# A graph layer on one Trainium2 core: a home in SBUF for every gathered tile, and other unit sizes for its features

## The chip, the cores and the metric

The kernel runs on 1 core of one Trainium2 chip. The time is device microseconds of one execution of the whole program. The engines are called PE (TensorE), DVE (VectorE), ACT (ScalarE), POOL (GpSimd) and SP (SyncE, here only a queue of plain DMAs).

## The reference, cut to what matters

`x` has 100,000 nodes of 32 floats. There are 25,000 edges, sorted by their destination `dst`.

```python
h = relu(layernorm(x))                         # 100000 x 32
# node part: a product of every node's own features
out = x + concat(h[:, :8] @ Ws, einsum(h[:, 8:], Wv)) / sqrt(8)
# edge part
w = silu(silu(edge_attr_8 @ W1 + b1) @ W2 + b2) @ W3 + b3   # 25000 x 256
hs_e, hv_e = h[src]                            # gather of source rows
messages = tensor_product(hs_e, hv_e, edge_attr_4, w)       # 25000 x 32
out += segment_sum(messages, dst) / 4          # scatter with add
```

## The kernel before

It has two stages, and every engine runs its own program, tied to the others by semaphores.

**Node stage.** 50 chunks (48 of 128 partitions x 16 rows, two smaller ones). SP loads a chunk of `x` (`load_x`) and stores its result (`store`), PE, ACT and DVE work on it in `node_step(c, base, ...)`. `base` is the step; from step 8 on the steps are in a hardware loop of 8. In step `base`, DVE takes row sums of chunk `base + 2` if `base` is odd, and finishes chunk `base - 2` (`node_rstd`, `node_scale`, `node_add`). Ahead of step 8 DVE also scales the weights and makes a few constants.

**Gathers.** The edges are 196 tiles of 128. POOL fetches the source rows of one tile with one indirect DMA (`gather`, line 320): 128 rows of 128 bytes of `x` into `xg`. DVE and ACT turn gathered rows into features, unit by unit, in the steps `feat_sum` (writes `gsum`), `feat_centre` (writes `gc`), `feat_square`, `feat_var`, `feat_std`, `feat_rstd`, `feat_scale` (writes `h_all`). There are three buffers `xg`, and POOL waits for the `feat_centre` of the unit that used a buffer before it fills it again (`gc_done`). Units 0 to 11 have 10 tiles each, and a unit is summed in node step 4n + 4. Unit 12 has 17 tiles and is summed in the last steps of the node stage. The other units have 5 tiles (the last has 4), one for each pass of the edge stage. POOL gathers 147 tiles ahead of its first scatter, and 49 between the scatters.

**Edge stage.** 12 passes of 4 quads and one more quad: 49 quads (q = 0 to 48), each of 4 tiles. PE makes the weights `w` of a quad, DVE multiplies and sums (`products`, `sum_vectors`, `sum_scalars`, `outer_product`, `vectors`), PE adds up rows with one destination within a quad (`sum_batch`), ACT copies these sums out of PSUM (`copy_sums`, line 508) into one of `NS` = 4 buffers `sums`, DVE works out which rows are written and where (`index_rank` to `index_out`, line 1038 writes `idx_i`), and POOL adds them to `out` in DRAM with 4 indirect DMAs (`scatter`, line 351). A scatter's first DMA waits for `idx_done` of its quad and for the landing of three DMAs of the quad before; the second waits for the landing of the fourth, and a `nop` then signals `landed`. `copy_sums(q)` waits for `landed >= q - 2`, so the work on the quads can be some three quads ahead of POOL. Between the scatters of a pass POOL gathers 1, 1, 1 and 2 tiles. It starts to scatter only when all chunks are stored.

**SP's queue** is in order. At lines 274 and 275 it waits for `dst_pad`, which an `iota` on POOL gives (line 335, behind the 20th gather), and only then come the store of `spare0`, the first `store` and the load of chunk 8.

Of the kernel before, what the change touches and what calls it, by code (L numbers as in the profile page):

```python
# [19 lines left out]
def gnn_layer(nc, x, src, dst, edge_sh, edge_radial, W1, b1, W2, b2, W3, b3, Ws, Wv, out):  # L20
# [6 lines left out]
    P = 128  # L27
# [36 lines left out]
    GT, GM, GL = 10, 17, 5  # L64
    GF = EARLY * GT + GM
    assert GF + GL * (NU // 2 - 1) + BT == T + 1
    DR = D + 1
    BW = BT * P
    HL = (NU // 2 - 2) // 2
# [9 lines left out]
    with ctx:  # L79
# [43 lines left out]
        xg = [sb(f"xg{i}", [P, GM * D]) for i in range(3)]  # L123
        gsum = sb("gsum", [P, GM])
        gc = sb("gc", [P, GM * D])
        gsq = sb("gsq", [P, GM * D])
        gvar = sb("gvar", [P, GM])
        gstd = sb("gstd", [P, GM])
        grstd = sb("grstd", [P, GM])
        h_all = sb("h_all", [P, (T + 1) * D])  # L130
# [32 lines left out]
        def bank(b, n=1):  # L163
# [20 lines left out]
            sum_ready sums_done scattered scattered_last idxc_done carry_done erlast_loaded dve_zero b3_scaled""".split()  # L184
# [4 lines left out]
        gathered = [sem(f"gathered{i}") for i in range(3)]  # L189
# [10 lines left out]
        def unit_first(n):  # L200

            return GF + (n - EARLY - 1) * GL

        def unit_slot(odd):
            return 1 if odd else 2

        def unit_count(half, odd):

            return half * GL + (EARLY // 2 * GT + GL if odd else GL)
# [5 lines left out]
        def _(sp):  # L215
# [85 lines left out]
            def edge_pass(v):  # L301
# [5 lines left out]
            edge_pass(0)  # L307
            with sp.Fori(1, NU // 2 - 1) as v:
                edge_pass(v)
# [3 lines left out]
        def _(pool):  # L313
# [5 lines left out]
            def gather(t, i, slot):  # L319
                pool.indirect_dma_start(xg[slot][:, i * D:(i + 1) * D], None, x,  # L320
                                        bass.IndirectOffsetOnAxis(ap=src_all[:, t:t + 1], axis=0))\
                    .then_inc(gathered[slot], 16)

            pool.wait_ge(src_loaded, 16)
            for n in range(EARLY):
                if n >= 2:

                    pool.wait_ge(s["gc_done"], n - 1)
                for i in range(GT):
                    gather(n * GT + i, i, n % 2)  # L330
                if n == 1:
                    pool.iota(rank_w[:, :], pattern=[[1, 1]], base=(127 + 63) << 23, channel_multiplier=-(1 << 23))\
                        .then_inc(s["pool_const"], 1)
                    pool.iota(trash_i[:, :], pattern=[[P, BT]], base=N, channel_multiplier=1).then_inc(s["pool_const"], 1)
                    pool.iota(dst_i[:, T:T + 1], pattern=[[1, 1]], base=N + (BT - 1) * P, channel_multiplier=1)\
                        .then_inc(s["dst_pad"], 1)
# [29 lines left out]
            def edge_pass(v):  # L366

                n, slot = EARLY + 3 + v, unit_slot(v % 2)
                t0 = unit_first(n)
                tiles = max(0, min(GL, T + 1 - t0))  # L370
                if tiles > 0:
                    if t0 + tiles > T:
                        pool.wait_ge(srclast_loaded, 16)

                    pool.wait_ge(s["gc_done"], n - 1)
                for k in range(4):
                    for i in range(k * tiles // 4, (k + 1) * tiles // 4):
                        gather(t0 + i, i, slot)
                    scatter(4 * v + k, 4 * v + k)


# [3 lines left out]
            for v in range(NU // 2):  # L385
                edge_pass(v)
            scatter(NQ - 1, NQ - 1)
# [5 lines left out]
        def _(act):  # L393
# [71 lines left out]
            def node_step(c, base, i):  # L465
# [6 lines left out]
                if 4 <= base < FULL:  # L472
                    n = 2 * i + base % 8 // 4 - 1
                    if base % 4 == 1:
                        feat_square(n, GT)
                    if base % 4 == 3:
                        feat_std(n, GT)

                if base == FULL:
                    feat_square(EARLY - 1, GT)  # L480
                if base == FULL + 2:
                    feat_square(EARLY, GM)
                if base == FULL + 1:
                    feat_std(EARLY - 1, GT)
# [61 lines left out]
            feat_std(EARLY, GM)  # L546
# [9 lines left out]
            def edge_pass(v, first, last):  # L556
                n = EARLY + 1 + v
                for h in range(2):
# [8 lines left out]
                    if h == 0 and not first:  # L567
                        feat_std(n - 1, GL)
# [4 lines left out]
                    if h == 1:  # L573
                        feat_square(n, BT if last else GL)
# [606 lines left out]
```

## Time and profile before

| | |
|---|---|
| median of 3 runs | 660.89 us (660.28 to 661.85) |
| time of the profiled execution | 658.62 us |
| its span, first to last instruction | 656.7 us |
| mean granted TensorE clock in it | 0.809 |
| busy, share of the span | PE 80%, DVE 71%, ACT 59%, POOL 77% |
| gathers, scatter DMAs | 196, 196 |

The profile records one execution. The span is what the trace shows; 1.9 us of the execution's time lie outside it. A share of busy time is an average over two stages with different limits, and the chain of work that ended last tells which engine held up the end.

### The profile page before, as it was taken

Reading aid. Unit: us, or ns where it says so; the run is one execution under the profiler, and the core shown is the slowest. Engines: PE = TensorE matmul, PEld = TensorE weight load, DVE = VectorE, ACT = ScalarE, POOL = GpSimd, SP = SyncE. Lnnn points to the kernel's source line nnn. Section 1 sums busy time; section 2 is a strip of 40 time slices with the busy share of each in tenths; the row PEclk is TensorE's granted clock in tenths of the full one; section 3 lists DMA queues with packets and bytes.
Section 4 is the critical chain, followed back from the end, with each engine's and each line's share of the span. In section 5 each row is a group of like instructions: output and inputs, shape, how many; then the busy total and the mean of one; then the engine's idle time right before and its main releaser. Section 6 shows DMA issues by size and latency. Waiting matters only on the chain.

```text
span 656.7 us, 10632 instructions
## 1 busy us (share of the span) xinstructions
PE 523.2 (80%) x2843; PEld 397.3 (60%) x2867; DVE 465.9 (71%) x1137; ACT 388.4 (59%) x1107; POOL 505.1 (77%) x401
## 2 busy tenths in 40 slices
PE   6989999889239999888988888879898788887400
PEld 4878887778115766565666566656575556665400
DVE  5759986877238999987687677767688776786400
ACT  3435555554137898957586766667576866587300
POOL 5777777777770688888888888888888888888884
PEclk9859999899559989897768678887768778888555
DMA  4376675554110122222222222222222222222221
GB/s 120 97 234 197 197 207 175 162 170 138 46 31 4 10 13 12 12 12 11 12 11 12 9 12 11 12 12 11 12 11 11 11 10 9 10 10 11 8 9 6
DMA packets 54364, 33.95 MB, mean 52 GB/s; under 512 B 37942, under 2 KB 41928, under 8 KB 54344
## 3 DMA queue, kind: packets, MB, share of 16 engines
q0 software_dynamic: 34496, 6.45, 18.4%
q1 hardware_dynamic: 19784, 27.28, 12.4%
q8 instruction: 7, 0.11, 0.1%
q14 instruction: 13, 0.11, 0.1%
q10 hardware_dynamic: 64, 0.00, 0.0%
HBM read 17.60 MB, written 16.08 MB: 51 GB/s over the span
## 4 chain that ended last, share of the span: by engine, by line
POOL 36%; DMA 17%; issue 11%; DVE 4%; ACT 1%; PE 1%; POOLq 0%; DVEq 0%; ACTq 0%
POOL out_dram L351 35%; DMA out_dram<-sums,idx_i 17%; POOL xg L320 2%; DVE red L1059 1%; DVE prod L1050 1%; DVE prod L1046 1%; PE ps L683 0%; DVE msg L1066 0%; PE ps L669 0%; ACT dsq L520 0%; ACT eq L542 0%; DVE h_all L913 0%; ACT L434 0%; ACT L451 0%; DVE gc L897 0%
## 5 line engine op out<-in xcount | busy, mean ns | idle before, releaser
L351 POOL DMA_INDIRECT out_dram<-sums,idx_i x196 | 307.1, 1567 | 60.9 <-issue 52.0
L320 POOL DMA_INDIRECT xg<-in_x_dram,src_all x196 | 197.0, 1005 | 83.0 <-issue 56.0
L736 PE MATMUL ps<-msg,eq 128*128 128x32 f32 (+1 forms) x980 | 138.9, 304 | 3.8 <-ACT sums L508 2.6
L736 PEld LDWEIGHTS ps<-msg,eq 128*128 128x128 f32 x980 | 138.4, 227 | 4.0 <-issue 2.7
L683 PE MATMUL ps<-w3blk,x 128*128 128x512 f32 x196 | 125.6, 729 | 3.5 <-issue 2.8
L1059 DVE TENSOR_REDUCE red<-prod 128x128 f32<-128x1024 f32 x49 | 97.7, 1994 | 0.1
L520 ACT ACTIVATE dsq<-ps,dcol 128x512 f32<-128x512 f32 x196 | 87.1, 537 | 0.2 <-PE ps L695 0.2
L508 ACT ACTIVATE sums<-ps 128x132 f32<-128x132 f32 x49 | 13.7, 279 | 123.5 <-POOLq L361 99.9
L683 PEld LDWEIGHTS ps<-w3blk,x 128*128 128x128 f32 x196 | 46.0, 246 | 46.1 <-issue 41.5
L542 ACT ACTIVATE eq<-dsq,onecol 128x384 f32<-128x384 f32 x147 | 73.5, 520 | 0.0
L635 PEld LDWEIGHTS ps<-ones_g,sqT 128*128 128x128 f32 x392 | 53.7, 205 | 24.3 <-issue 17.1
L695 PEld LDWEIGHTS ps<-ident,dcol 128*128 128x128 f32 x196 | 23.8, 145 | 70.8 <-issue 59.0
L695 PE MATMUL ps<-ident,dcol 128*128 128x128 f32 x196 | 32.3, 290 | 42.1 <-ACT dsq L520 42.0
L1014 DVE SCALAR_TENSOR_TENSOR first<-sums,rank_max,dmt_all 128x4 f32<-128x4 f32 x49 | 10.7, 219 | 70.2 <-ACT sums L508 70.0
L639 PE MATMUL ps<-wself,rT 128*128 128x128 f32 x392 | 59.6, 298 | 0.0
L635 PE MATMUL ps<-ones_g,sqT 128*128 128x4 f32 x392 | 50.6, 252 | 9.9 <-ACT nstd L425 4.8
L417 ACT ACTIVATE sqT<-ps 128x512 f32<-128x512 f32 (+2 forms) x50 | 29.2, 584 | 42.4 <-PE ps L624 42.4
L1046 DVE TENSOR_TENSOR prod<-ps,coef 128x768 f32<-128x768 f32 x49 | 46.8, 954 | 10.2 <-PE ps L684 7.4
L1050 DVE TENSOR_TENSOR prod<-ps,coef 128x256 f32<-128x256 f32 x147 | 52.6, 413 | 0.0
L1066 DVE TENSOR_REDUCE msg<-prod 128x32 f32<-128x512 f32 x49 | 52.5, 1072 | 0.0
L639 PEld LDWEIGHTS ps<-wself,rT 128*128 128x128 f32 x392 | 50.9, 203 | 0.0
L669 PE MATMUL ps<-x,w2blk 128*128 128x512 f32 (+1 forms) x50 | 43.8, 973 | 3.3 <-ACT x L451 3.2
(102 smaller groups left out, 798.7 us busy)
## 6 DMA issues: line engine op xcount, KB each, us to landing
xin<-in_x_dram SPq DMA_DIRECT2D x48, 256.0 KB
out_dram<-oc SPq DMA_DIRECT2D x48, 256.0 KB, 2.1
xg<-in_x_dram,src_all POOLq DMA_INDIRECT x196, 2.4
out_dram<-sums,idx_i POOLq DMA_INDIRECT x196, 3.1
er<-in_edge_attr_dram SPq DMA_DIRECT2D x24, 32.0 KB
sh_all<-in_edge_attr_dram SPq DMA_DIRECT2D x1, 390.0 KB
xin<-in_x_dram SPq DMA_DIRECT2D x1, 192.0 KB
out_dram<-oc SPq DMA_DIRECT2D x1, 192.0 KB
```

The source lines that it names most:

```text
L320: pool.indirect_dma_start(xg[slot][:, i * D:(i + 1) * D], None, x, bass.IndirectOffsetOnAxis(ap=src_all[:, t:t + 1], axis=0))\
L351: pool.indirect_dma_start(out, bass.IndirectOffsetOnAxis(ap=idx_i[:, k % NS, a:a + 1], axis=0), sums[:, k % NS, a * DR:a * DR + D], None, ...
L520: m = act.activation(dsq[:, b * BW:b * BW + (BT - b) * P], psDT[:, b * P:BW], ACT.Square, bias=dcol[:, k % NS, b:b + 1], scale=-1.0)
L542: m = act.activation(e[:, o], dsq[:, o], ACT.Relu, bias=onecol[:, :], scale=-4.0, accum_out=lcnt[:, k % NS, b:b + 1])
L635: m = pe.matmul(psV[base % 2][0:p, 4 * g:4 * g + 4], sqT[:, base % 2, g * P:g * P + p], ones_g[:, :], start=True, stop=True)
L639: m = pe.matmul(psY[base % 2][0:p, g * P:(g + 1) * P], rT[:, base % 2, g * P:g * P + p], wself[:, :], start=True, stop=True)
L683: pe.matmul(o, x2[:, k // 2 % 2, j * P:(j + 1) * P], w3blk[:, :], start=True, stop=False)
L695: m = pe.transpose(psDT[:, b * P:(b + 1) * P], dcol[:, k % NS, b:b + 1].to_broadcast([P, P]), ident[:, :])
L736: m = pe.matmul(psSUM[:, a * DR:a * DR + n], eq[:, k % 2, o:o + P], msg[:, k % 2, b, 0:n], start=(b == a), stop=(b == a - 1 and (a < BT - ...
L1046: dve.tensor_tensor(prod[:, :, 0:192].rearrange("p t (g w) -> p t g w", w=MUL), w[:, :, 0:192].rearrange("p t (g w) -> p t g w", w=MUL), c ...
L1050: m = dve.tensor_tensor(prod[:, :, 192 + 64 * i:256 + 64 * i].rearrange("p t (g w) -> p t g w", w=MUL), w[:, :, 192:256].rearrange("p t (g ...
L1059: dve.tensor_reduce(red[:, :, :, :], prod[:, :, 128:384].rearrange("p t (g u w) -> p t g w u", u=MUL, w=MUL), X, ALU.add).then_inc(s["red_ ...
```

## The change

- `xg` is one tensor with a place for each of the 196 tiles (and a spare one), so no gather waits for a buffer. Twelve units of 10 tiles (`GT`) are made in the node stage, and 11 units of 7 tiles (`GL`) in the first 11 of the 12 edge passes; the unit of 17 and the last, smaller unit are gone.
- POOL gathers 164 tiles (`GA`) ahead of the first scatter, and one tile ahead of each of the scatters 0 to 31. Unit n of the first twelve still waits, now for `gsum_done` of unit n - 2, because two semaphores are used in turn.
- In the node stage a unit is summed and centred two steps later (step 4n + 6), and the steps after that follow one to four steps later than before.
- In the edge stage DVE waits for `late_landed`, which SP gives by a `nop` once all tiles of a unit have landed.
- SP loads the source indices ahead of the first two chunks. POOL makes its constants by `iota` ahead of the gathers.

```diff
-    GT, GM, GL = 10, 17, 5
-    GF = EARLY * GT + GM
+    GT, GL, GA = 10, 7, 164
+    GF = EARLY * GT
+    LATE = NU // 2 - 1
-        xg = [sb(f"xg{i}", [P, GM * D]) for i in range(3)]
+        xg = sb("xg", [P, (T + 2) * D])
...
+            sp.dma_start(src_all[:, 0:T], src_main).then_inc(src_loaded, 16)
             for c in range(2):
                 load_x(c, c)
-            sp.dma_start(src_all[:, 0:T], src_main).then_inc(src_loaded, 16)
...
+            for v in range(LATE):
+                sp.wait_ge(gathered_late[v], 16 * len(late_tiles(v)))
+                sp.nop(nofuse=True).then_inc(s["late_landed"], 1)
                 for h in range(2):
                     sp.wait_ge(s["erT_ready"], 2 * v + h + 1)
                     load_er(2 * v + 2 + h, h)
...
+            def gather(t):
+                if t == T:
+                    pool.wait_ge(srclast_loaded, 16)
+                signal = gathered[t // GT % 2] if t < GF else gathered_late[(t - GF) // GL]
+                pool.indirect_dma_start(xg[:, t * D:(t + 1) * D], None, x,
+                                        bass.IndirectOffsetOnAxis(ap=src_all[:, t:t + 1], axis=0)).then_inc(signal, 16)
             pool.wait_ge(src_loaded, 16)
             for n in range(EARLY):
                 if n >= 2:
-                    pool.wait_ge(s["gc_done"], n - 1)
-                for i in range(GT):
-                    gather(n * GT + i, i, n % 2)
+                    pool.wait_ge(s["gsum_done"], n - 1)
+                for t in range(n * GT, (n + 1) * GT):
+                    gather(t)
+            for t in range(GF, GA):
+                gather(t)
-            pool.wait_ge(s["gc_done"], EARLY - 1)
-            for i in range(GM):
-                gather(EARLY * GT + i, i, 0)
-            for i in range(GL):
-                gather(GF + i, i, 2)
-            pool.wait_ge(s["gc_done"], EARLY)
-            for i in range(GL):
-                gather(GF + GL + i, i, 1)
...
-            for v in range(NU // 2):
-                edge_pass(v)
-            scatter(NQ - 1, NQ - 1)
+            for q in range(NQ):
+                if GA + q <= T:
+                    gather(GA + q)
+                scatter(q, q)
...
-                centring = 4 <= base <= FULL and base % 4 == 0
-                scaling = centring and base >= 8
+                centring = base % 4 == 2 and base >= 6
+                scaling = centring and base >= 10
```

POOL's program at its start. Before (`gc_done` and `gsum_done` are signals of DVE, `src_loaded` is that of the source indices):

```order
L316 AFFINE_SELECT ident<-ident 128x128
L320 DMA xg<-in_x_dram,src_all 128x32 [waits src_loaded]
L320 DMA xg<-in_x_dram,src_all 128x32 x19
L332 IOTA rank_w 128x1
L334 IOTA trash_i 128x4
L335 IOTA dst_i 128x1
L320 DMA xg<-in_x_dram,src_all 128x32 [waits gc_done]
L320 DMA xg<-in_x_dram,src_all 128x32 x9
```

Now:

```order
L307 AFFINE_SELECT ident<-ident 128x128
L310 IOTA rank_w 128x1
L312 IOTA trash_i 128x4
L313 IOTA dst_i 128x1
L320 DMA xg<-in_x_dram,src_all 128x32 [waits src_loaded]
L320 DMA xg<-in_x_dram,src_all 128x32 x19
L320 DMA xg<-in_x_dram,src_all 128x32 [waits gsum_done]
L320 DMA xg<-in_x_dram,src_all 128x32 x9
```

The three `iota`, on the last of which SP's queue waits, moved from behind the 20th gather to ahead of the first.

DVE's program in node steps 8 and 9, before (the three node instructions of step 8 and what a feature unit adds to it, then the row sums of step 9):

```order
L909 RECIPROCAL grstd<-gstd 128x10 [waits gstd_done]
L890 REGISTER_ALU
L891 TENSOR_REDUCE gsum<-xg 128x10 [waits gathered1]
L857 ISA
L858 RECIPROCAL nrstd<-nstd 128x16 [waits std_done]
L913 ISA [waits grstd_done]
L913 SCALAR_TENSOR_TENSOR h_all<-gc,grstd 128x320
L867 TENSOR_TENSOR oc<-ps,nrstd 128x512 [waits rstd_done,y_ready]
L897 SCALAR_TENSOR_TENSOR gc<-gsum,xg 128x320 [waits h_done,gsum_done]
L874 TENSOR_TENSOR oc<-oc,xin 128x512 [waits y_used]
```

Now steps 8 and 9, up to the sum of unit 1 in step 10:

```order
L820 RECIPROCAL nrstd<-nstd 128x16 [waits std_done]
L864 ISA
L865 TENSOR_REDUCE gvar<-gsq 128x10 [waits gsq_done]
L829 TENSOR_TENSOR oc<-ps,nrstd 128x512 [waits rstd_done,y_ready]
L836 TENSOR_TENSOR oc<-oc,xin 128x512 [waits y_used]
L797 ISA
L798 TENSOR_REDUCE nsum<-xin 128x16 [waits x_loaded3]
L820 RECIPROCAL nrstd<-nstd 128x16 [waits std_done]
L806 REGISTER_ALU [waits xT_ready]
L807 SCALAR_TENSOR_TENSOR xc<-nsum,xin 128x512 [waits xsum_done]
L829 TENSOR_TENSOR oc<-ps,nrstd 128x512 [waits rstd_done,y_ready]
L836 TENSOR_TENSOR oc<-oc,xin 128x512 [waits y_used]
```

The sum of unit 1, for which POOL's 31st gather waits, moved from the start of step 8 to the start of step 10.

## Rows read from the trace of the kernel before

**Rows 1.** The page: busy time, DMA share of 40 slices in tenths, and the last chain.
```profile
PE 523.2 (80%) x2843; PEld 397.3 (60%) x2867; DVE 465.9 (71%) x1137; ACT 388.4 (59%) x1107; POOL 505.1 (77%) x401
...
DMA  4376675554110122222222222222222222222221
...
POOL 36%; DMA 17%; issue 11%; DVE 4%; ACT 1%; PE 1%; POOLq 0%; DVEq 0%; ACTq 0%
```

**Rows 2.** POOL's timeline, start and length in us: gathers, then scatters.
```profile
4.61 1.15 POOL L320 DMA_INDIRECT xg<-in_x_dram,src_all  x1 [3.12 <-DMA src_all<-in_src_dram]
...
43.80 1.15 POOL L320 DMA_INDIRECT xg<-in_x_dram,src_all  x1 [0.97 <-DVE gc L897]
...
196.42 0.94 POOL L320 DMA_INDIRECT xg<-in_x_dram,src_all  x1 [0.30 <-issue]
217.57 0.94 POOL L320 DMA_INDIRECT xg<-in_x_dram,src_all  x1 [20.21 <-DVE gc L897]
218.81 1.62 POOL L351 DMA_INDIRECT out_dram<-sums,idx_i  x1 [0.30 <-issue]
```

**Rows 3.** POOL's timeline: the first DMA of scatters 1, 2, 40 and 48.
```profile
227.66 1.58 POOL L351 DMA_INDIRECT out_dram<-sums,idx_i  x1 [0.30 <-DMA out_dram<-sums,idx_i]
...
236.45 1.57 POOL L351 DMA_INDIRECT out_dram<-sums,idx_i  x1 [0.30 <-issue]
...
582.04 1.55 POOL L351 DMA_INDIRECT out_dram<-sums,idx_i  x1 [0.40 <-issue]
...
642.43 1.55 POOL L351 DMA_INDIRECT out_dram<-sums,idx_i  x1 [0.30 <-issue]
```

**Rows 4.** ACT's waits: for whom, us in all, times, longest.
```profile
ACT sums L508 <- POOLq L361: 99.9, 36, 4.7
```

**Rows 5.** DVE's timeline: `index_rank` at the scatters' start, and nine quads later.
```profile
220.01 0.21 DVE L1014 SCALAR_TENSOR_TENSOR first<-sums,rank_max,dmt_all 128x4 f32<-128x4 f32 x1
...
284.48 0.21 DVE L1014 SCALAR_TENSOR_TENSOR first<-sums,rank_max,dmt_all 128x4 f32<-128x4 f32 x1
```

**Rows 6.** DVE's timeline at the end of the node stage.
```profile
186.22 0.72 DVE L891 TENSOR_REDUCE gsum<-xg 128x17 f32<-128x544 f32 x1 [15.25 <-DMA xg<-in_x_dram,src_all]
...
190.64 0.34 DVE L995 TENSOR_TENSOR dotp<-h_all,sh_all 128x192 f32<-128x192 f32 x1
```

**Rows 7.** SP's queue: issue times, and its wait for POOL's `iota`.
```profile
0.75 0.88 SPq L225 DMA_DIRECT2D xin<-in_x_dram  x2
1.67 0.43 SPq L235 DMA_DIRECT2D src_all<-in_src_dram  x1
...
32.09 0.37 SPq L225 DMA_DIRECT2D xin<-in_x_dram  x1
...
SPq L275 <- POOL dst_i L335: 6.7, 1, 6.7
```

**Rows 8.** PE's and DVE's timelines around node steps 7 to 10.
```profile
35.99 1.11 PE L609 MATMUL ps<-ident,xin 128*128 128x128 f32 x4 [4.53 <-DMA xin<-in_x_dram]
...
32.67 0.41 DVE L829 CAST b3lo<-b3r 1x512 bf16<-1x512 f32 x1
37.55 0.69 DVE L836 TENSOR_REDUCE nsum<-xin 128x16 f32<-128x512 f32 x1 [4.47 <-DMA xin<-in_x_dram]
...
49.19 0.25 DVE L858 RECIPROCAL nrstd<-nstd 128x16 f32<-128x16 f32 x1 [1.25 <-ACT nstd L425]
```

**Rows 9.** DVE's timeline: the row sums that open steps 9, 13 and 21.
```profile
44.06 0.68 DVE L836 TENSOR_REDUCE nsum<-xin 128x16 f32<-128x512 f32 x1
...
56.86 0.68 DVE L836 TENSOR_REDUCE nsum<-xin 128x16 f32<-128x512 f32 x1
...
79.01 0.68 DVE L836 TENSOR_REDUCE nsum<-xin 128x16 f32<-128x512 f32 x1
```

**Rows 10.** POOL's gathers in groups, 50 to 98 us and 130 to 163 us.
```profile
L320 POOL DMA_INDIRECT xg<-in_x_dram,src_all x35 | 38.2, 1091 | 10.7 <-issue 10.7
...
L320 POOL DMA_INDIRECT xg<-in_x_dram,src_all x27 | 25.7, 951 | 8.2 <-issue 8.2
```

More of the change, by code:

```diff
@@ L188, in gnn_layer @@
         src_loaded, src_pad, srclast_loaded = sem("src_loaded"), sem("src_pad"), sem("srclast_loaded")
-        gathered = [sem(f"gathered{i}") for i in range(3)]
+        gathered = [sem(f"gathered{i}") for i in range(2)]
+        gathered_late = [sem(f"gathered_late{i}") for i in range(LATE)]
         er_loaded = [sem(f"er_loaded{i}") for i in range(2)]
@@ L364, in scatter @@
                 tile(0, s["scattered_last"])
[L366 to L379, printed above, removed]
             for k in range(XS):
@@ L566, in edge_pass @@
                     dst_square(q + 1, kq + 1)
-                    if h == 0 and not first:
-                        feat_std(n - 1, GL)
+                    if h == 0:
+                        feat_std(n - 1, GT if first else GL)
                     if not end:
@@ L572, in edge_pass @@
                     dst_equal(q + 1, kq + 1)
-                    if h == 1:
-                        feat_square(n, BT if last else GL)
+                    if h == 1 and not last:
+                        feat_square(n, GL)
                     copy_sums(q, kq)
@@ L938, in node_step @@
                 if centring:
-                    feat_sum(n, slot, count, w)
+                    odd = base % 8 == 2
+                    dve.wait_ge(gathered[odd], (i if odd else i + 1) * (16 * GT))
+                    feat_sum(n, n * GT, GT)
                 if out_too:
@@ L1083, in _, with edge_pass @@
             dve.wait_ge(s["sh_loaded"], 32)
-            def edge_pass(v, half, odd, first, last):
-                n = EARLY + 1 + v
-                fw = BT if last else GL
-                was = EARLY * GT if first else unit_first(n - 1)
-                ww = GM if first else GL
-                slot = unit_slot(odd)
-                count = 16 * (unit_count(half, odd) - (GL - BT if last else 0))
+            def edge_pass(v, first, last):
+                n = EARLY + v
+                t0 = GF + v * GL
+                was, ww = ((EARLY - 1) * GT, GT) if first else (t0 - GL, GL)
                 for h in range(2):
@@ L1105, in edge_pass @@
                         products(q, k, u)
-                        if h == 1 and r == 0:
-                            feat_sum(n, slot, count, fw)
+                        if h == 1 and r == 0 and not last:
+                            dve.wait_ge(s["late_landed"], v + 1)
+                            feat_sum(n, t0, GL)
                         if ready:
@@ L1110, in edge_pass @@
                         sum_vectors(q, k)
-                        if h == 1 and r == 0:
-                            feat_centre(n, slot, fw)
+                        if h == 1 and r == 0 and not last:
+                            feat_centre(n, t0, GL)
                         if ready:
                             index_later(q - 2, k - 2)
-                        if h == 0 and r == 0 and not first:
+                        if h == 0 and r == 0:
                             feat_var(n - 1, ww)
```

111 lines of the change are left out of this document (37 added, 74 removed).

## The prediction

> **What bounds the kernel now.** The page first. PE is the busiest engine, but in the chain that ended last it has 1%, while POOL has 36%, DMAs 17% and issue 11% [rows 1]. So POOL's own timeline comes next. It has two stretches. From 4.61 us to 197 us it issues 147 gathers, then it idles 20.21 us until DVE has centred a unit, and from 218.81 us on it issues scatters and gathers with the usual 0.30 us between two instructions [rows 2, 3]. Is the second stretch really POOL's, or is the edge work just as slow? The waits of ACT tell: the copy of a quad's sums waits 99.9 us in all for POOL's `landed` signal, 36 times [rows 4]. POOL holds up the others. And where the others run free they are quicker: DVE makes nine quads from 220.01 to 284.48 us, 7.16 us each [rows 5], while POOL takes 8.79 us from scatter 1 to scatter 2 [rows 3].
>
> The distances between scatters give the price of a gather that stands there. Scatter 1 to 2 holds one and takes 8.79 us; the last eight distances hold none and take (642.43 - 582.04) / 8 = 7.55 us each [rows 3]. All 48 distances take 642.43 - 218.81 = 423.6 us and hold 48 gathers, so a gather costs (423.6 - 48 x 7.55) / 48 = 1.28 us; the single distance gives 1.24.
>
> At the seam of the stages DVE waits 15.25 us for the 17 tiles of unit 12 and starts the edge stage at 190.64 us [rows 6].
>
> **The scatter stretch after the change.** 31 gathers stand between scatter 0 and scatter 48 in place of 48. That is 17 x 1.28 = 21.8 us less: 423.6 - 21.8 = 401.8 us. From scatter 32 on there is none, so 17 distances in a row must keep to 7.55 us, where before there were nine. DVE's free pace of 7.16 us is below that. Two more tiles in the unit of a pass add to it: 0.72 us for 17 tiles of `gsum` [rows 6] is 0.04 us a tile, for four such instructions and two tiles 0.3 us a pass of four quads, under 0.1 us a quad. Work on quads can also run three quads ahead, and a lag would have to use that up first. With this cover I cost the larger units at nothing; without it they would cost 12 x 0.3 = 4 us.
>
> **The gather stretch.** All of it lies on POOL's chain, so I rebuild its start and length.
> - Start. The source indices are issued at 1.67 us, now ahead of the two loads that start at 0.75 [rows 7]: 0.9 us earlier. The first gather moves from 4.61 [rows 2] to about 3.7 us. The `iota` fit in the 3.12 us for which POOL waits there.
> - Length. From the first to the 147th gather it was 191.8 us [rows 2]. Of this 0.67 us was the wait at 43.80 (0.97 less the usual 0.30), and some 0.2 us the three `iota` (an estimate: they are three short instructions between two gathers). This leaves 190.9 us. The slower pace of the middle (35 gathers in 48.9 us, 1.40 each, against 27 in 33.9, 1.26 each, later [rows 10]) is in it, and I keep it.
> - From the 147th gather to scatter 0: 18 more gathers at 1.28 = 23.0 us, and 1.24 us from the last of them to the scatter (217.57 to 218.81 [rows 2]). The 20.21 us of idle time go, and this work takes their place.
> - Sum: 3.7 + 190.9 + 23.0 + 1.24 = 218.8 us, the very time at which scatter 0 starts now. The 17 gathers fill the hole, no more and no less.
>
> **The wait that could grow.** The 31st gather waits for the sum of unit 1, which moves from node step 8 to step 10. In the old trace step 10 starts at 47.9 us (49.19 less 1.25 of idle [rows 8]); the sum would end at about 48.6 and POOL go on at 48.9, though ready at 42.0 (43.80 - 0.67 - 0.9 - 0.2). That would be 6.9 us of new stall. But those steps are late for a reason that the change removes. SP's queue waits 6.7 us for the last `iota`, so the load of chunk 8 is issued only at 32.09 us [rows 7], and PE waits 4.53 us and DVE 4.47 us for `xin` [rows 8]. With the `iota` in front, that load goes out at about 25.4 us. DVE then enters step 7 when its weight work ends, at 33.1 us, not at 37.55 [rows 8], 4.45 us earlier. Step 9 starts at 44.06 [rows 9] less 4.45, less some 0.9 us for the unit's work that leaves step 8: 38.7 us. It took 3.9 us (44.06 to 47.9), of which I take 0.9 for waits on a slow PE (an estimate, from the 1.25 us in step 10): 3.0 us. So the sum of unit 1 runs from 41.7 to 42.2 us, POOL is ready at 42.0 and waits about 0.3 us. Later units are safe: four node steps take 11.1 us ((79.01 - 56.86) / 2 [rows 9]) and ten gathers 12.6 to 14, so DVE gets ahead. I add 0.3 us, and scatter 0 starts at 219.1.
>
> **Costs that lie beside.** Unit 11's last gather starts at about 160 us (3.7 + 119 x 191.8 / 146) and lands some 3 us later; the edge stage starts 4.4 us after that (186.22 to 190.64 [rows 6]), at 168 us in place of 190.64. These 22 us are worth nothing: the four buffers of sums are full by about 200 us, and then all wait for POOL. `late_landed` goes through SP's queue, behind the `er` loads of the pass before; the last tile of a late unit is gathered eight quads or more ahead of its use, so its wait is costed at nothing. Without that cover DVE would wait for the landing of gathers in each of 11 passes. Scatter 0 also waits for all stores, which end with the node stage.
>
> **Sum.** 219.1 + 401.8 + (656.7 - 642.43 = 14.3, the last scatter, its landing and the end) = 635.2 us of span against 656.7: 21.5 us less. The profiled execution took 658.62 us and gives 637.1; it lies 2.3 us below the median of the runs, 660.89, and against that median the forecast is 639.4 us.
>
> **The lock on POOL's port.** A scatter's DMA takes 1.57 to 1.58 us beside a busy DVE (227.66, 236.45) and 1.55 when DVE has ended (642.43) [rows 3]: no slowing. Gathers do slow in 50 to 98 us [rows 10], and 44 of them (121 to 164) now run beside the edge stage, where DVE used to be idle. If DVE is what slows them, they cost 44 x (1.40 - 1.26) = 6 us more. If the load of the DMA engines is, nothing: it is 5 to 7 tenths there, 4 around 160 us and 0 to 2 in the edge stage [rows 1]. The Trainium skill, "SBUF — State Buffer", section "Who interferes with whom", says that GpSimd is shut out of a port pair for the whole of a `copy`, `cast` or `tensor_scalar` that runs in a two-port mode, while a `tensor_reduce` never contends on this chip. By this rule the edge stage, which is mostly reduces and products out of PSUM, would slow the gathers by next to nothing, and the sum would stay; a kernel with many such copies beside its gathers would pay.
>
> **The rivals.**
> - *The step-10 stall stays* (chance 0.12). Something else than chunk 8 makes steps 7 to 10 late, for instance the work on PE. Then the stall is 6.9 and not 0.3 us: 646 us. Against it: both engines name `xin` in rows 8.
> - *Gathers beside the edge stage are slow* (0.10), as worked out: 639.4 + 6 = 645.5 us.
> - *The edge work is the bound from scatter 32 on* (0.04). If quads need 8.8 us there, 17 x 1.25 = 21 us are missing, less the lead of about 16 us (three distances of 7.55 less some 6 from the copy to the indices): 644.5 us. Against it: ACT's waits and the 7.16 us.
> - *POOL is starved, and the kernel gets slower* (0.04). At each of the 44 gathers where DVE used to be idle, POOL waits behind one of DVE's instructions. The gain is used up at 21.5 / 44 = 0.49 us each, a pace of 1.77 us, beyond even the 1.40 of rows 10. Behind instructions of 1 us each it would be 44 us more: 683 us. Against it: the scatters of rows 3.
> - *The gathers get quicker* (0.04). Spread otherwise over a node stage with fewer stalls, a part of the 35 x 0.14 = 5 us by which they lag in the middle goes: 635.5 us.
>
> **How the numbers follow.** The forecast has 0.66, with its own range of 637 to 642.5 us (first gather and stall 1 us either way, price of a gather 1.24 to 1.28, units of seven 1 us, and the spread of the runs, 0.8 us either way). The range of 8 in 10 reaches to the rivals near it on the slow side and takes part of the quick one: 636 to 647 us. About 0.2%, 1.3 us, is what a measurement of this kernel can tell from no change. All cases but the starved POOL are faster by more than that, 0.96; of its 0.04 about 0.01 falls within 0.2%, and 0.03 is slower.
>
> **What the new profile would show.** Right: a first gather near 3.7 us; chunk 8 loaded near 25 us and no wait of PE for `xin` there; no idle time of POOL over 1 us until scatter 0, which starts at 217.5 to 220.5 us; distances of 8.8 us up to scatter 31 and 7.55 after; ACT still waiting for POOL to the end. Wrong: a stall of POOL between 42 and 49 us; gathers at 1.4 us beyond 165 us; scatters among the last 17 that wait for `idx_i`.

## The result and the profile after the change

| | before | after |
|---|---|---|
| median | 661.16 us (660.28 to 661.85, 4 runs) | 642.11 us (640.1 to 644.92, 4 runs) |
| profiled execution, span | 658.62, 656.7 us | 642.62, 640.8 us |
| mean granted TensorE clock | 0.809 | 0.822 |

The changed kernel takes 0.9728 of the time (95% interval 0.969 to 0.9766), 19 us less. Forecast were 639.4 us, with a likeliest range of 637 to 642.5 us, in which the time lies at the upper end.

First the page of the changed kernel: busy time, the chain that ended last, and two groups of instructions.

```profile
PE 516.0 (81%) x2843; PEld 391.3 (61%) x2867; DVE 466.7 (73%) x1128; ACT 388.9 (61%) x1104; POOL 506.3 (79%) x401
...
POOL 60%; issue 18%; DMA 16%; SPq 2%; DVE 2%; PE 1%; ACTq 0%; ACT 0%; POOLq 0%; DVEq 0%
...
L337 POOL DMA_INDIRECT out_dram<-sums,idx_i x196 | 306.6, 1564 | 64.6 <-issue 55.4
L320 POOL DMA_INDIRECT xg<-in_x_dram,src_all x196 | 198.8, 1014 | 62.3 <-issue 59.1
```

POOL now has 60% of the chain where it had 36% [rows 1]: the part that ran over DVE and the node stage is gone, and nearly all of the span is POOL's instructions, the 0.30 us between them and the landing of its DMAs. Its waits and ACT's, from the chain of waits of the changed kernel (us in total, times, longest):

```profile
POOL xg L320 <- DVE gsum L852: 1.8, 1, 1.8
...
ACT sums L471 <- POOLq L347: 119.3, 42, 11.1
```

The 20.21 us of [rows 2] have no successor. ACT waits for POOL 42 times instead of 36 [rows 4]: POOL is the bound still, and more so. POOL's timeline gives the places to set against [rows 2, 3]: the first gather, the 30th and 31st, the 147th, the 165th (which stands just ahead of scatter 0), scatters 0 and 1, the first DMAs of the scatters 44 and 45, the last DMA of scatter 45, and the first DMAs of the scatters 46 and 48.

```profile
3.10 1.16 POOL L320 DMA_INDIRECT xg<-in_x_dram,src_all  x1 [1.36 <-DMA src_all<-in_src_dram]
...
41.77 0.95 POOL L320 DMA_INDIRECT xg<-in_x_dram,src_all  x1 [0.30 <-issue]
44.55 0.95 POOL L320 DMA_INDIRECT xg<-in_x_dram,src_all  x1 [1.83 <-DVE gsum L852]
...
198.13 0.95 POOL L320 DMA_INDIRECT xg<-in_x_dram,src_all  x1 [0.30 <-issue]
...
220.89 0.95 POOL L320 DMA_INDIRECT xg<-in_x_dram,src_all  x1 [0.30 <-issue]
222.15 1.63 POOL L337 DMA_INDIRECT out_dram<-sums,idx_i  x1 [0.30 <-issue]
...
231.01 1.57 POOL L337 DMA_INDIRECT out_dram<-sums,idx_i  x1 [0.30 <-DMA out_dram<-sums,idx_i]
...
595.74 1.55 POOL L337 DMA_INDIRECT out_dram<-sums,idx_i  x1 [0.50 <-issue]
...
603.35 1.55 POOL L337 DMA_INDIRECT out_dram<-sums,idx_i  x1 [0.49 <-issue]
...
608.92 1.55 POOL L337 DMA_INDIRECT out_dram<-sums,idx_i  x1 [0.30 <-issue]
611.66 1.55 POOL L337 DMA_INDIRECT out_dram<-sums,idx_i  x1 [1.19 <-issue]
...
626.93 1.55 POOL L337 DMA_INDIRECT out_dram<-sums,idx_i  x1 [0.48 <-issue]
```

The scatters 44 and 45 start 7.61 us apart (595.74, 603.35), but 45 and 46 8.31 us (603.35, 611.66), with 1.19 us of "issue" before the later one.

The terms of the sum, predicted and measured in the profiled execution:

| term | predicted | measured | from |
|---|---|---|---|
| first gather | 3.7 | 3.10 | timeline |
| wait before the 31st gather | 0.3 | 1.53 | 1.83 less 0.30 |
| 1st to 147th gather without that wait | 190.9 | 193.5 | 198.13 - 3.10 - 1.53 |
| 147th gather to scatter 0 | 24.2 | 24.02 | 222.15 - 198.13 |
| scatter 0 starts | 219.1 | 222.15 | |
| scatter 0 to scatter 48 | 401.8 | 404.78 | 626.93 - 222.15 |
| the end | 14.3 | 13.87 | 640.8 - 626.93 |
| span | 635.2 | 640.8 | |

So three small terms make the 5.6 us: the gathers' pace (2.6), the stall (1.2) and the scatter stretch (3.0), less 0.6 and 0.4 at the two ends. In the medians the miss is 642.11 - 639.4 = 2.7 us. That it is only half as large is luck: the profiled execution before was 2.3 us shorter than its median and the forecast added them back, while the one after was 0.5 us longer than its own (642.62 against 642.11).

**The scatter stretch.** Its 31 distances with one gather have a mean of 8.817 us (31 distances from 222.15 us), as before. The 17 without have 7.73 us, not 7.55. Four of them, 34 to 35, 39 to 40, 42 to 43 and 45 to 46, take 8.14, 8.35, 7.99 and 8.31 us.

**The stall.** The load of chunk 8 goes out at 25.32 us (predicted 25.4). DVE enters step 7 at 32.75 (33.1) and reaches the row sums of step 9 at 38.65 (38.7). Up to there the working holds. Then it waits. The timelines of SP, PE and DVE:

```profile
25.32 0.37 SPq L219 DMA_DIRECT2D xin<-in_x_dram  x1
```

```profile
36.15 1.08 PE L570 MATMUL ps<-ident,xc 128*128 128x128 f32 x4 [4.54 <-ACT rT L389]
```

```profile
32.75 0.67 DVE L798 TENSOR_REDUCE nsum<-xin 128x16 f32<-128x512 f32 x1
...
38.65 0.67 DVE L798 TENSOR_REDUCE nsum<-xin 128x16 f32<-128x512 f32 x1
40.78 0.25 DVE L820 RECIPROCAL nrstd<-nstd 128x16 f32<-128x16 f32 x1 [1.47 <-ACT nstd L396]
...
42.39 0.69 DVE L829 TENSOR_TENSOR oc<-ps,nrstd 128x512 f32<-128x512 f32 x1 [0.73 <-PE ps L600]
...
43.85 0.43 DVE L852 TENSOR_REDUCE gsum<-xg 128x10 f32 x1
```

ACT's timeline shows why it is late itself:

```profile
32.86 0.61 ACTq L459 DMA_DIRECT2D b3rows<-b3mid  x1
33.50 0.60 ACTq L460 DMA_DIRECT2D b3rows<-b3lo  x1
34.43 0.60 ACT L373 ACTIVATE xTs<-ps 128x512 f32<-128x512 f32 x1 [5.78 <-issue]
```

PE no longer waits for `xin`, but it stands 4.54 us all the same, now for ACT, and step 9 pays 1.47 + 0.73 = 2.2 us for being ahead of it. ACT issues two DMAs of split weights (`b3rows`) behind its step 7, and they wait for DVE's `b3lo`, which ends at 32.82 us (32.41 + 0.41, the weight work behind which DVE enters step 7). Only then, at 34.43 us, does ACT go on with the next chunk. Before the change the same two issues stood at 33.12 and 33.76 us, and the late chunk 8 hid them. The sum of unit 1 runs at 43.85, not at 41.7.

### The profile page after: what moved, and what is told of

The parts are those of the page before. It is cut to its first block, busy times and chain, and to the rows that moved or that the text cites. A ratio compares the mean times of both kernels' runs of the same rounds, so it can differ in the third digit from the quotient of the medians.

```text
span 640.8 us, 10596 instructions
## 1 busy us (share of the span) xinstructions
PE 516.0 (81%) x2843; PEld 391.3 (61%) x2867; DVE 466.7 (73%) x1128; ACT 388.9 (61%) x1104; POOL 506.3 (79%) x401
## 4 chain that ended last, share of the span: by engine, by line
POOL 60%; issue 18%; DMA 16%; SPq 2%; DVE 2%; PE 1%; ACTq 0%; ACT 0%; POOLq 0%; DVEq 0%
POOL out_dram L337 38%; POOL xg L320 21%; DMA out_dram<-sums,idx_i 14%; DMA xin<-in_x_dram 1%; PE ps L600 0%; PE ps L596 0%; DMA wself<-in_L_gnn_Wv_dram 0%; DVE oc L829 0%; SPq L239 0%; DMA wself<-wself 0%; PE ps L585 0%; PE ps L570 0%; SPq L234 0%; SPq L259 0%; DVE oc L836 0%
## 5 line engine op out<-in xcount | busy, mean ns | idle before, releaser
L697 PE MATMUL ps<-msg,eq 128*128 128x32 f32 (+1 forms) x980 | 135.1, 299 | 5.6 <-ACT sums L471 5.6
L697 PEld LDWEIGHTS ps<-msg,eq 128*128 128x128 f32 x980 | 134.5, 222 | 5.8 <-issue 5.8
L388 ACT ACTIVATE sqT<-ps 128x512 f32<-128x512 f32 (+2 forms) x50 | 29.3, 585 | 43.7 <-PE ps L585 42.2
L630 PE MATMUL ps<-x,w2blk 128*128 128x512 f32 (+1 forms) x50 | 41.4, 923 | 6.3 <-ACT x L422 6.1
```

The costliest lines, as they stand in the source:

```text
L697: m = pe.matmul(psSUM[:, a * DR:a * DR + n], eq[:, k % 2, o:o + P], msg[:, k % 2, b, 0:n], start=(b == a), stop=(b == a - 1 and (a < BT - ...
```

## The experiments

Four kernels ran beside the kernel before at 659.40 us (657.51 to 660.79, 13 runs). Their ratios are to that.

**1. 147 gathers ahead of the first scatter.** Theory A is that POOL's total work sets the end, wherever a gather stands; theory B that moving 17 gathers into the stretch brings their time back.

```diff
-    GT, GL, GA = 10, 7, 164
+    GT, GL, GA = 10, 7, 147
...
-                if GA + q <= T:
-                    gather(GA + q)
+                for _ in range(2 if q < ahead else 1):    # ahead = 17
+                    if t <= T:
+                        gather(t)
+                        t += 1
```

> The changed kernel, but with 147 tiles gathered ahead of the first scatter as before the change, and two tiles ahead of each of the scatters 0 to 16, one ahead of 17 to 31, none after. Theory A (POOL never idles now, so only the total of its work counts, not where the gathers stand): the first scatter moves from 222.2 to about 200.5 us, the scatter stretch grows from 404.8 to about 426.5 us, and the time stays at 642 us, 640 to 645. Theory B (the gain comes from taking 17 gathers out of the scatter stretch): the time goes back by 17 x 1.28 = 22 us, to about 663 us.

Measured: 645.4 us (644.64 to 646.65), ratio 0.9784 (0.9758 to 0.9809). Its timeline at the seam:

```profile
203.11 0.95 POOL L320 DMA_INDIRECT xg<-in_x_dram,src_all  x1 [0.30 <-issue]
204.36 1.63 POOL L337 DMA_INDIRECT out_dram<-sums,idx_i  x1 [0.30 <-issue]
...
212.11 1.03 POOL L320 DMA_INDIRECT xg<-in_x_dram,src_all  x1 [0.31 <-issue]
213.44 0.97 POOL L320 DMA_INDIRECT xg<-in_x_dram,src_all  x1 [0.30 <-DMA out_dram<-sums,idx_i]
214.72 1.62 POOL L337 DMA_INDIRECT out_dram<-sums,idx_i  x1 [0.30 <-issue]
```

Scatter 0 starts 17.8 us earlier than in the changed kernel, and the stretch is 426.5 us and so 21.7 longer: 16 distances with two gathers take 10.17 us each, 15 with one 8.84, 17 with none 7.71. (One more gather than before the edit stands ahead of scatter 0, so 16 gathers and not 17 move into the stretch.) So the total is what counts, but for 3.9 us by which the sum of both is above the changed kernel's. 2.5 of them arise ahead of the 147th gather (200.60 for 198.13 us), where POOL waited 5.3 us for `gsum` in three waits instead of 1.8 in one. The other 1.4 are the price of the 16 gathers: 21.7 us between the scatters, 20.3 ahead of them. The median lies just above theory A's 640 to 645 us and far from the 663 us of theory B, which falls. So 164 is not what makes the kernel faster. What does is that POOL has work for the time in which it idled.

**2. The three `iota` behind the 20th gather, as before.**

```diff
-            pool.iota(rank_w, ...); pool.iota(trash_i, ...); pool.iota(dst_i, ...)
             pool.wait_ge(src_loaded, 16)
             for n in range(EARLY):
                 ...
+                if n == 1:
+                    pool.iota(rank_w, ...); pool.iota(trash_i, ...); pool.iota(dst_i, ...)
```

> The changed kernel with POOL's three constants made behind the 20th gather again, so that SP's queue waits for the last of them as before. Theory A (node steps 7 to 10 were late only because chunk 8 was loaded late): PE and DVE wait some 4 us for xin near 33 us, the sum of unit 1 ends at about 48.5 us, POOL idles some 6 us ahead of its 31st gather in place of 1.8 us, and the time is about 5 us longer, 647 us. Theory B (those steps have their own pace): the stall stays at 1.8 us and the time at 642 us.

Measured: 642.75 us (642.28 to 643.99), ratio 0.9752 (0.9725 to 0.9778). The waits for `xin` came back, 3.6 us of PE and 3.4 of DVE, and so did a stall, 4.2 us. Yet scatter 0 starts at 222.07, where the changed kernel's starts at 222.15. The expected 5 us did not come: the 31st gather is at 45.94 instead of 44.55 us, and the rest up to scatter 0 takes 176.1 instead of 177.6. Neither theory has this: the waits went the way of A, the time that of B. The remaining gathers went quicker here, and the section on the prediction takes that up.

**3. POOL's wait without DVE.** POOL waits for the landing of unit n - 2, not for its sum.

```diff
-                    pool.wait_ge(s["gsum_done"], n - 1)
+                    pool.wait_ge(gathered[n % 2], 16 * GT * (n // 2))
```

> The changed kernel, but POOL waits ahead of unit n for the landing of unit n - 2 in place of its sum by DVE, which keeps the two semaphores unambiguous. Theory A (the 31st gather's wait for the sum lies on the chain): POOL's 1.8 us stall near 42 us goes, the first scatter starts 1.5 us earlier at about 220.6 us, and the time is 640.6 us. Theory B (POOL would only run into another wait, for instance for DMA queue room): the stall moves and the time stays at 642.1 us.

Measured: 642.58 us (641.19 to 643.46), ratio 0.9749 (0.9723 to 0.9775). The stall is gone, as these two rows of its timeline show against 41.77 and 44.55 above:

```profile
41.68 0.95 POOL L320 DMA_INDIRECT xg<-in_x_dram,src_all  x1 [0.30 <-issue]
42.93 1.45 POOL L320 DMA_INDIRECT xg<-in_x_dram,src_all  x1 [0.30 <-issue]
```

Scatter 0 starts at 220.26 us (1.9 earlier), the span is 639.1 (1.7 shorter). So in this execution the stall was on the chain, as theory A says. In the medians it can't be told from the changed kernel, whose ratios are 0.9728 and, in experiment 8, 0.9754.

**4. The kernel before with the new start alone** (source indices first, `iota` first).

```diff
+            sp.dma_start(src_all[:, 0:T], src_main).then_inc(src_loaded, 16)
             for c in range(2):
                 load_x(c, c)
-            sp.dma_start(src_all[:, 0:T], src_main).then_inc(src_loaded, 16)
...
+            pool.iota(rank_w, ...); pool.iota(trash_i, ...); pool.iota(dst_i, ...)
             def gather(t, i, slot):
...
-                if n == 1:
-                    pool.iota(rank_w, ...); pool.iota(trash_i, ...); pool.iota(dst_i, ...)
```

> The kernel before with the start of the change alone: the source indices loaded ahead of the first chunks, and POOL's three constants made ahead of the gathers. Theory A (the gathers and the buffers decide the node stage's end): the first gather moves from 4.6 to about 3.1 us, the 20 us hole ahead of the first scatter stays, and the time is 1 to 2 us shorter, about 659.5 us. Theory B (the late load of chunk 8 was a large part of the loss before): the edge stage starts some 5 us or more earlier and the time is 655 us or less.

Measured: 658.22 us (655.77 to 659.34, 10 runs), ratio 0.9979 (0.9963 to 0.9996). The first gather starts 1.6 us earlier, but the hole stays, since DVE's centring ends it:

```profile
196.00 0.95 POOL L326 DMA_INDIRECT xg<-in_x_dram,src_all  x1 [0.31 <-issue]
216.55 0.95 POOL L326 DMA_INDIRECT xg<-in_x_dram,src_all  x1 [19.60 <-DVE gc L897]
```

The early start is worth 1.2 us, and the other 18 of the 19 us come from the rest of the change: a home for each tile, the order of the gathers, and the unit sizes that go with it. No run takes these apart.

**5. Short stores.** What slows the gathers between 50 and 110 us? Theory A says the DMA load. Each store of the node stage writes 32 of its 512 columns.

```diff
-                sp.dma_start(v, oc[0:p, base % XS, 0:n]).then_inc(stored[base % XS], 16)
+                sp.dma_start(v[:, 0:D], oc[0:p, base % XS, 0:D]).then_inc(stored[base % XS], 16)
```

> The changed kernel with a sixteenth of each node chunk's store left out of nothing but the first row group: only 32 of the 512 columns of a chunk are stored, so most of the output is missing. Theory A (gathers slow down where the load of the DMA engines is high): between 50 and 110 us the load falls by nearly half and the gathers' pace from 1.38 towards 1.30 us or less; the first scatter starts some 3 us or more earlier. Theory B (DVE's instructions with two operands in SBUF slow POOL's descriptor work): the pace stays at 1.38 us.

**6. Short centring.** Theory B says DVE's long instruction on two operands in SBUF, the centring of a chunk. That of the odd chunks covers 2 of 16 row groups.

```diff
+            dve.memset(xc[:, :, :], 0.0)
...
-  dve.scalar_tensor_tensor(out=xc[0:p, k, 0:r * D]..., in0=nsum[0:p, k, 0:r]..., in1=xin[0:p, base % XS, 0:r * D]...)
+  w = 2
+  dve.scalar_tensor_tensor(out=xc[0:p, k, 0:w * D]..., in0=nsum[0:p, k, 0:w]..., in1=xin[0:p, base % XS, 0:w * D]...)
```

> The changed kernel with the centring of the odd node chunks cut to 2 of 16 row groups (the rest of xc is zero, so the node output of odd chunks is wrong). DVE's scalar_tensor_tensor on xin and nsum takes about 0.15 us in place of 0.69. Theory B (this instruction, with both operands in SBUF, holds up POOL): the pace of the gathers between 50 and 110 us falls from 1.38 to about 1.28 us, and the first scatter starts 4 to 5 us earlier, near 218 us. Theory A (the DMA load does it): the pace stays at 1.38 us.

**7. Landing wait and 157 gathers ahead**, the edit of 3 with GA = 157: if POOL's total is all that counts, seven gathers may stand later.

> The changed kernel with POOL's wait for the landing of unit n - 2 in place of its sum, and with 157 tiles gathered ahead of the first scatter, one ahead of each of the scatters 0 to 38. Theory A (a gather between two scatters covers part of the wait for the landing of a scatter; without one the distance is 7.73 us, with one 8.82 less 1.28 = 7.54): seven more scatters are covered, 7 x 0.19 = 1.3 us, and the stall of 1.8 us goes: 3 us less than the changed kernel, 639 us. Theory B (a distance costs the same with and without): 1.5 us less, 640.6 us.

**8. The changed kernel once more**, unedited, beside them.

> The changed kernel once more, unchanged, beside the kernel below on one chip. By both theories 0.973 of the kernel before. It is timed to see how far its runs spread (640.1 to 644.9 us at first, against 660.3 to 661.9 before): if the stall of the 31st gather differs from run to run, this kernel spreads by 3 us or more.

These four ran on a chip on which the kernel before itself takes 757.13 us (753.83 to 764.25, 11 runs). Nothing of theories A and B can be read there: 786.61 us (5), 789.72 (6), 815.25 (7; 813.34 to 818.23) and 773.59 (8; 754.72 to 787.26). What that chip shows stands in the last section. They were run again on chips on which the kernel before takes 659.97 us (median of 11 runs each time).

> The kernel of e5 once more: of each node chunk only 32 of 512 columns are stored, so most of the output is missing. Theory A (the load of the DMA engines slows the gathers): the pace between 50 and 110 us falls from 1.38 to 1.30 us or less. Theory B (DVE's instructions slow them): it stays at about 1.38 us.

Measured: 647.38 us in one run. Between 50 and 110 us the core moves 109 GB/s instead of 198, yet the 30 gathers from the 41st on take 41.7 us (from 60.0 us on), and in the changed kernel 41.7 us too (from 58.06 on). With little more than half the traffic the pace is the same, so theory A falls.

> The kernel of e6 once more, since that run fell on a chip where plain DMAs crawl beside gathers: the centring of the odd node chunks is cut to 2 of 16 row groups, so their node output is wrong. Theory B (DVE's scalar_tensor_tensor with both operands in SBUF holds up POOL): the gathers' pace between 50 and 110 us falls from 1.38 to about 1.28 us and the first scatter starts near 218 us in place of 222. Theory A (the DMA load does it): the pace stays at 1.38 us.

Measured: 645.78 us in one run. The same 30 gathers, from 58.66 us on, take 40.5 us, 1.2 us less than in the changed kernel. The forecast 1.28 us did not come: the pace is 1.35 us for 1.39. This one instruction is a part, not the whole. What lies behind the slow gathers is read below, instruction by instruction.

> The changed kernel once more, unchanged. 0.973 of the kernel before if this chip is like the first one. If the stall of the 31st gather differs from run to run, its runs spread by 3 us or more. Were the crawl of plain DMAs beside gathers general, it would come out slower than before here too, as it did on the last chip (773.6 against 757.1 us).

Measured: 643.51 us (642.22 to 645.76, 6 runs), ratio 0.9754 (0.9729 to 0.9779). In its profiled execution POOL waits 5.5 us for `gsum` in three waits, 3.69 of them ahead of the 31st gather, and scatter 0 starts at 223.95. So POOL's waits differ between executions of one program, 1.8 and 5.5 us, and the runs spread by 3.5 us. Plain DMAs don't crawl here.

> The kernel of e8 once more: POOL waits for the landing of unit n - 2 in place of its sum, 157 tiles are gathered ahead of the first scatter and one ahead of each of the scatters 0 to 38. Theory A (a gather between two scatters covers part of the wait for a scatter's landing): ten distances without a gather in place of 17, 7 x 0.19 = 1.3 us less, and the stall near 42 us gone, 1.5 us less; the ratio to before is 0.969. Theory B (the cover does nothing): 0.971. If plain DMAs crawl beside gathers on this chip, it is slower than the kernel before, and by more than the changed kernel was, since here DVE does not hold POOL back.

Measured: 649.07 us (646.07 to 649.71, 6 runs), ratio 0.9837 (0.981 to 0.9865), 5.6 us above the changed kernel, where the theories gave 0.969 and 0.971, and so 3 to 4 us below it. Scatter 0 starts at 211.94 us, as seven gathers less than in experiment 3 give (220.26 - 7 x 1.255 = 211.5), but scatter 39 comes 13.44 us after 38. With that, nothing can be read of the cover that A and B are about. In order: the timelines of POOL, SP, PE, ACT and DVE of this kernel.

```profile
546.30 1.02 POOL L320 DMA_INDIRECT xg<-in_x_dram,src_all  x1 [0.30 <-issue]
...
561.07 1.63 POOL L337 DMA_INDIRECT out_dram<-sums,idx_i  x1 [6.29 <-DVE idx_i L992]
```

```profile
549.46 0.80 SPq L211 DMA_DIRECT2D er<-in_edge_attr_dram  x2
```

```profile
551.26 0.47 PE L618 MATMUL ps<-ident,er 128*128 128x128 f32 x1 [24.36 <-DMA er<-in_edge_attr_dram]
```

```profile
556.49 0.28 ACT L471 ACTIVATE sums<-ps 128x132 f32<-128x132 f32 x1 [4.37 <-PE ps L703]
```

```profile
556.93 0.22 DVE L968 SCALAR_TENSOR_TENSOR first<-sums,rank_max,dmt_all 128x4 f32<-128x4 f32 x1 [24.61 <-ACT sums L471]
```

The last gather is issued at 546.30. SP's queue waits for its landing before it signals `late_landed`, and behind that stand the two loads of `er` (edge attributes), which leave at 549.46. PE, in order too, waited 24.36 us for them with the sums of quad 39 behind, and ACT, DVE and POOL follow. The lead that hid this in the changed kernel is measured by its absence: there the last gather starts at 494.17 us, seven scatters earlier, and no scatter waits for `idx_i`.

## Why the prediction came out as it did

**POOL is the bound; 17 gathers fill the hole.** Right, and shown by experiments 1 and 4. The 147th gather to scatter 0 took 24.02 us (24.2), and the stretch lost 18.8 of the 21.8 us.

**The wait at the 31st gather** was mis-sized, 1.5 for 0.3 us. The step that failed: step 9 was given 3.0 us, on the thought that with chunk 8 early the waits on PE go. It took 5.1 us (38.65 to 43.7), 2.2 of it such waits. PE started late because ACT did, which stood at its two DMA issues for DVE's weight work, a wait that the prediction had not seen behind that for `xin`. It is the rival "the step-10 stall stays" in weak form: the wait ahead of the 31st gather was 1.83 us here and 3.5 to 3.7 in four other executions of this order (experiments 1, 5 and 6, and the repeat), about half of the 6.9 us. In experiment 3 and in the repeat the shift of the 31st gather reached scatter 0 whole (1.6 us earlier and 1.9; 1.3 us later and 1.8). Of the signs named ahead, this stall is one of "wrong", and scatter 0 at 222.15 us lies outside 217.5 to 220.5.

**Distances without a gather** were mis-sized, 7.73 for 7.55 us: 17 x 0.18 = 3.1 us. My row held the eight last distances, and 7.43 to 7.65 us was all they showed. The chance of a bound edge stage (0.04) is not it: no scatter waits for `idx_i`, and among the last 17 the trace names "issue" alone. 39 to 40, 42 to 43 and 45 to 46 are long (7.87 to 8.40 us) in every run that keeps the changed kernel's order there: experiments 1 to 3, 5 and 6, and the repeat. In the kernel before the same three take 7.55, 7.64 and 7.47 us, on the same data, and in experiment 7, with seven gathers moved, other distances are long (8.63 us for 39 to 40, 8.00 for 41 to 42 and 46 to 47). So they belong to places in POOL's program. The landings are not late there: by the trace's records the third DMA of a scatter lands 1.4 to 1.6 us after its end in long and short distances alike, and the next scatter starts 0.75 us after that landing, but 1.21 us in 42 to 43 and 1.49 in 45 to 46 (1.21 and 1.50 in the repeat). In 39 to 40 the extra time, 1.48 for 0.79 us, lies ahead of the scatter's second DMA. POOL itself takes longer at these places; why stays open.

**The gathers' pace** was mis-sized by 2.6 us. In groups, for 50 to 98 us and 130 to 163 us of the changed kernel:

```profile
L320 POOL DMA_INDIRECT xg<-in_x_dram,src_all x35 | 37.5, 1071 | 10.7 <-issue 10.7
```

```profile
L320 POOL DMA_INDIRECT xg<-in_x_dram,src_all x26 | 26.1, 1004 | 7.9 <-issue 7.9
```

The middle is as before or a little quicker (1071 for 1091 ns), but 130 to 163 us has slow gathers that weren't there (1004 for 951 ns [rows 10]). By number: from the 31st gather to the 111th both kernels take 107.0 us; the first 29 distances take 1.6 us more than before without its `iota` (38.67 for 37.07), and the 111th to the 147th 0.9 more (46.5 for 45.6). Two things lie in it, and two of the experiments tell which part of the change brings them.

The first is the gather that nothing disturbs. The 147 gathers by line, with least, median and greatest length in ns, in this order: the kernel before, the changed kernel, experiment 2 (the whole change, but `iota` late) and experiment 4 (the kernel before, but the new start).

```profile
L320 POOL DMA_INDIRECT xg<-in_x_dram,src_all x147: 940/945/1396, 4.6 to 196.4; - x147
```

```profile
L320 POOL DMA_INDIRECT xg<-in_x_dram,src_all x147: 947/952/1433, 3.1 to 198.1; - x147
```

```profile
L315 POOL DMA_INDIRECT xg<-in_x_dram,src_all x147: 940/945/1397, 3.1 to 198.3; - x147
```

```profile
L326 POOL DMA_INDIRECT xg<-in_x_dram,src_all x147: 947/952/1446, 3.0 to 196.0; - x147
```

With the three `iota` ahead of the gathers the median gather takes 7 ns more, 1.0 us in 146. All the other kernels with this order have the same 7 ns (medians of 952 to 954). Why is open.

The second is which gathers are slow, and that can be read from two timelines side by side, POOL's and DVE's of the changed kernel:

```profile
69.17 1.26 POOL L320 DMA_INDIRECT xg<-in_x_dram,src_all  x1 [0.31 <-issue]
70.74 1.09 POOL L320 DMA_INDIRECT xg<-in_x_dram,src_all  x1 [0.30 <-issue]
72.13 1.02 POOL L320 DMA_INDIRECT xg<-in_x_dram,src_all  x1 [0.30 <-issue]
73.46 0.95 POOL L320 DMA_INDIRECT xg<-in_x_dram,src_all  x1 [0.30 <-issue]
```

```profile
68.92 0.69 DVE L836 TENSOR_TENSOR oc<-oc,xin 128x512 f32<-128x512 f32 x1
...
70.31 0.69 DVE L807 SCALAR_TENSOR_TENSOR xc<-nsum,xin 128x512 f32<-128x512 f32 x1
...
71.64 0.69 DVE L836 TENSOR_TENSOR oc<-oc,xin 128x512 f32<-128x512 f32 x1
...
73.39 0.67 DVE L829 TENSOR_TENSOR oc<-ps,nrstd 128x512 f32<-128x512 f32 x1
```

A normal gather takes 0.95 us. The one at 69.17 starts 0.44 us before DVE's L836 ends (68.92 + 0.69 = 69.61) and is 0.31 us longer. The one at 70.74 starts 0.26 before the end of L807 and is 0.14 longer; at 72.13 it is 0.20 and 0.07. At 73.46 DVE is inside an instruction as long, but one that reads PSUM and one operand in SBUF, and the gather takes 0.95. All 29 gathers above 0.99 us between 50 and 130 us start inside a DVE instruction with two operands in SBUF, and each is longer by the rest of it less 0.12 us, to within 0.02. The same holds for the 21 of experiment 6 and the 35 of experiment 5. Two kinds of gathers that start in such an instruction stay at 0.95 us: those with less than 0.13 us of it left, and those that start together with it. At 133.54 us both start at once; the gather takes 0.95 us and DVE's L836 0.72 instead of 0.69. It also fits both experiments: the store has no part in it, and of the instructions with two such operands only one was cut, in every second chunk. Among the 30 gathers from the 41st on, that centring (L807) lengthened 8 in the changed kernel, by 2.3 us, and none in experiment 6; others took up a part, so that 1.2 us were left. It is the Trainium skill, "SBUF — State Buffer", section "Who interferes with whom", that says of such an instruction that it contends with a GpSimd instruction that reads SBUF, because its second input comes through the shared read interface; a gather reads its indices. The trace agrees. The prediction had weighed that section's other rule, on two-port modes, and took from it that gathers beside the edge stage would cost nothing. That held (40 gathers between 165 and 215 us, median 952 ns), so the rival of 6 us falls. It took the slow gathers over as a fixed pace of the middle, when each depends on where it starts against DVE. Over the whole stretch two-operand instructions cost 8.3 us before and 9.4 in the changed kernel. With the 1.0 us above, and 0.4 from five gathers beside other DVE instructions, this makes the 2.6 us nearly whole.

It is the new start that shifts them, and not the moved feature steps. Without POOL's waits and the `iota`, the 1st to the 147th gather take 190.9 us before and 193.5 in the changed kernel. Experiment 2, which has the moved steps but not the early `iota`, takes 191.1 (195.21 less 3.93 and 0.18). Experiment 4, which has the new start but the old steps, takes 192.9. Other executions with the new start take 192.3 (the repeat) to 195.3 us (experiment 5), so its size differs from one to the next. The prediction credited the early `iota` with the saved stall and put no price on the gathers behind it. The two cancel: experiment 2 reaches scatter 0 at 222.07 us, the changed kernel at 222.15.

One reading of the prediction doesn't hold by itself: a scatter DMA of 1.55 us was taken as one beside a DVE that has ended, but at 585.75 us of the kernel before one takes 1.55 us too, and DVE is at work.

**Start, unit sizes, `late_landed`.** The first gather came 1.5 us earlier (0.9 forecast). The larger units cost nothing; distances with a gather are 8.82 us as before. The wait through SP's queue cost nothing, as forecast. Experiment 7 shows what it costs when the last gather comes seven scatters later: one distance of 13.44 us.

## What to carry to other kernels

When an in-order engine bounds a kernel, add up its instructions and its gaps. A change that gives it work for a gap is worth that work, almost wherever in the sequence it stood, until a gather comes too late for the queue behind its signal (SP's loads here). When a wait is taken away, look on every engine for the one that stood behind it (ACT's DMA issues here). In these runs a DVE instruction with two operands in SBUF lengthened an indirect DMA that POOL began inside it by what was left of it. So a shift of a few us at the start changes what all later gathers meet, and a pace from one trace is good to 1 to 3 us in 190. A price read from eight distances was good to 2.4% for seventeen (7.55 and 7.73 us).

## What the runs showed of the hardware

On one chip the same programs were far slower: the kernel before 757.13 for 660 us, the changed one 773.59 (754.72 to 787.26). The gathers are not what is slow there. Windows of 40 us of experiment 7's kernel on that chip (us, then busy time and count of PE, PEld, DVE, ACT, POOL, PE's clock, DMA share, GB/s):

```profile
100.00:140.00 40.00, 7.72 (x26) 5.42 (x26) 0.25 (x1) 1.85 (x4) 30.25 (x33) 0.50 0.10 14
260.00:300.00 40.00, 39.68 (x304) 35.04 (x304) 35.84 (x77) 23.79 (x59) 0.00 (x0) 1.00 0.59 188
```

The changed kernel on the first chip, in the first of these windows:

```profile
100.00:140.00 40.00, 37.68 (x274) 32.40 (x273) 29.86 (x64) 21.25 (x53) 30.54 (x32) 0.96 0.62 185
```

POOL issues its gathers at full pace (33 in 40 us), and the plain loads and stores of the node stage get 14 GB/s beside them, in place of 185 for all. With POOL done (260 to 300 us) the node stage runs at 188 GB/s. POOL then waited 158.2 us for the stores. In the changed kernel on that chip POOL waited 101.9 us for `gsum` in ten waits, and this wait shares out the time: between 100 and 140 us POOL issues 18 gathers and the core moves 112 GB/s. So the gate whose cost can't be told from nothing in the medians of experiment 3 is the likely reason why the changed kernel is quicker than that of experiment 7 there, 754.72 to 787.26 us against 813.34 to 818.23. It isn't shown by itself, since that kernel also has 157 gathers for 164. Why plain DMAs starve there is open.
